# GNN layer, output stage: TensorE's waits of a block gathered in one place, layer 2 with 512 moving columns

## The reference

```python
msgs_f = mlp2(concat(h[src], h[dst], edge), W1_f, b1_f, W2_f, b2_f)
msgs_r = mlp2(concat(h[dst], h[src], edge), W1_r, b1_r, W2_r, b2_r)
agg = segment_sum(msgs_f, dst) + segment_sum(msgs_r, src)
out = x + h + relu(concat(agg, h) @ Wn1 + bn1) @ Wn2 + bn2
```

## Time and profile before

| | us |
|---|---|
| time before, median of 3 executions (1595.52 to 1598.82) | 1595.94 |
| the profiled execution's own time | 1595.95 |
| its span, first to last instruction | 1594.2 |
| output stage, first table transpose to the end of the span | 1341.1 to 1594.2 |
| TensorE busy over the span | 1280.9 (80%) |

### The profile page before, as it was taken

How to read it: one execution, slowest core, us unless ns; L and a number is a source line. 1 busy time by engine, 2 the same in 40 slices (tenths; PEclk the granted TensorE clock), 3 DMA queues, 4 the chain that set the end, 5 groups by cost and what they waited for, 6 DMA issues and landing times.

```text
span 1594.2 us, 29478 instructions
## 1 busy us (share of the span) xinstructions
PE 1280.9 (80%) x7070; PEld 969.6 (61%) x7070; DVE 970.8 (61%) x3294; ACT 942.6 (59%) x2256; POOL 1102.0 (69%) x1003
## 2 busy tenths in 40 slices
PE   5998998557888787878777788778678873999998
PEld 4777776335666565666555566556566652777776
DVE  7999999526666666666666666666666650222222
ACT  4888888434555455555455555555555442777776
POOL 7888888888888888888888888888888863000000
PEclk9999999767777888787888877877977786999999
DMA  6899998535555555555555555555555545999998
GB/s 217 292 315 315 314 315 279 161 49 111 111 112 111 111 99 102 104 104 103 105 105 105 105 104 99 106 102 99 101 102 105 104 78 156 382 370 369 364 367 297
DMA packets 238410, 281.00 MB, mean 176 GB/s; under 512 B 53170, under 2 KB 155200, under 8 KB 238348
## 3 DMA queue, kind: packets, MB, share of 16 engines
q1 hardware_dynamic: 168408, 241.57, 45.3%
q0 software_dynamic: 68992, 38.59, 21.5%
q10 hardware_dynamic: 948, 0.30, 0.1%
HBM read 162.62 MB, written 117.72 MB: 176 GB/s over the span
## 4 chain that ended last, share of the span: by engine, by line
POOL 36%; issue 21%; PE 18%; DMA 2%; DVE 1%; POOLq 1%; ACT 0%; ACTq 0%; DVEq 0%; SPq 0%
POOL table L532 30%; PE bank L871 6%; PE bank L882 6%; POOL got_odd L514 6%; PE bank L892 3%; DMA table<-to_send,scatter_at 2%; PE bank L820 1%; PE bank L846 1%; PE bank L818 1%; DVE same L979 0%; PE bank L833 0%; DMA same<-table 0%; ACT nh L639 0%; ACT to_send L625 0%; POOLq L530 0%
## 5 line engine op out<-in xcount | busy, mean ns | idle before, releaser
L532 POOL DMA_INDIRECT table<-to_send,scatter_at x392 | 623.5, 1591 | 134.7 <-issue 117.8
L846 PEld LDWEIGHTS bank<-message,same 128*128 128x128 f32 x1960 | 279.1, 229 | 45.6 <-issue 40.4
L846 PE MATMUL bank<-message,same 128*128 128x128 f32 x1960 | 300.2, 320 | 5.0 <-DVE message L1011 5.0
L639 ACT ACTIVATE nh<-nx,all_sums,all_rstd 128x64 f32<-128x64 f32 x784 | 280.3, 434 | 0.0
L514 POOL DMA_INDIRECT got_even<-in_x,gather_first x196 | 211.8, 1080 | 40.2 <-issue 35.0
L775 PE MATMUL bank<-wn_h,nturned 128*128 128x256 f32 x784 | 197.0, 395 | 31.7 <-ACT nhidden L683 24.1
L514 POOL DMA_INDIRECT got_odd<-in_x,gather_at x180 | 180.3, 1002 | 54.9 <-issue 54.9
L804 PE MATMUL bank<-ident,h_ends 128*128 128x128 f32 x196 | 51.4, 355 | 200.5 <-DVE h_ends L1020 185.6
L979 DVE TENSOR_SCALAR_CACHE_REDUCE same<-others,ids 128x128 f32<-128x128 int32 (+3 forms) x392 | 190.8, 543 | 12.7 <-DVE ids L971 7.5
L818 PE MATMUL bank<-turned,w_ends 128*128 128x256 f32 x392 | 167.8, 518 | 34.8 <-ACT turned_edge L609 34.8
L775 PEld LDWEIGHTS bank<-wn_h,nturned 128*128 128x128 f32 x784 | 143.5, 193 | 67.7 <-issue 37.9
(11 more groups left out here) (80 smaller groups left out, 1999.2 us busy)
## 6 DMA issues: line engine op xcount, KB each, us to landing
nx<-in_x SPq DMA_DIRECT2D x194, 256.0 KB
table<-nhidden SPq DMA_DIRECT2D x97, 512.0 KB
same<-table SPq DMA_DIRECT2D x97, 512.0 KB, 5.3
others<-numbers SPq DMA_DIRECT2D x196, 128.0 KB
out_x<-nh SPq DMA_DIRECT2D x79, 256.0 KB, 4.4
nx<-out_x SPq DMA_DIRECT2D x55, 256.0 KB, 4.4
out_x<-ncentred SPq DMA_DIRECT2D x49, 256.0 KB, 4.2
table<-to_send,scatter_at POOLq DMA_INDIRECT x392
```

The source lines that it names most:

```text
L532: pool.indirect_dma_start(table, bass.IndirectOffsetOnAxis(ap=scatter_at[s][:, k:k + 1], axis=0), to_send[s][:, k, :], None, compute_op=AL ...
L639: last = act.activation(nh[s][:, g, :], nx[place][:, g, :], ACT.Relu, bias=all_sums[:, at, g:g + 1].rearrange("p a g -> p (a g)"), scale=a ...
L846: last = pe.matmul(bank[6 + s][:, k * M:(k + 1) * M], same[s][:, o, k * P:(k + 1) * P], message[s][:, o, :], start=(o == k), stop=(o == KB ...
```

## The change

Nothing but TensorE's program of the output stage is changed. The table transposes of a block are now written at the end of the step before it, all waits of a step stand in front of the back transposes, and the second layer takes 512 moving columns in two matmuls where it took 256 in four. The first table transposes stand ahead of the loop.

```diff
             def turn_table(i, s, turn, place):
-                pe.wait_ge(n_tab[place], 16 * (turn + 1))
-                if not first(i):
-                    pe.wait_ge(n_hidden[s], 2 * i)
                 for odd in range(2):
...
             def layer2_nodes(i, s):
-                if not first(i):
-                    pe.wait_ge(n_biased[s], i)
-                pe.wait_ge(n_hidden[s], 2 * (i + 1))
-                for c in range(0, 512, 256):
-                    for odd in range(2):
-                        last = pe.matmul(bank[s][odd * D:(odd + 1) * D, c:c + 256], wn2[:, :],
-                                         nhidden[s][:, odd * 512 + c:odd * 512 + c + 256], start=True, stop=True)
+                for odd in range(2):
+                    last = pe.matmul(bank[s][odd * D:(odd + 1) * D, :], wn2[:, :],
+                                     nhidden[s][:, odd * 512:(odd + 1) * 512], start=True, stop=True)
                 last.then_inc(n_l2[s], 1)

             def turn_back(i, s):
-                pe.wait_ge(n_biased[s], i + 1)
-                if not first(i):
-                    pe.wait_ge(n_out[s], i)
                 for q in range(G // 2):
...
+            def wait_biased(i, s):
+                pe.wait_ge(n_biased[s], i + 1)
+                if not first(i):
+                    pe.wait_ge(n_out[s], i)
+
+            def wait_hidden(i, s):
+                pe.wait_ge(n_hidden[s], 2 * (i + 1))
+
+            def wait_table(i, s, turn, place):
+                pe.wait_ge(n_tab[place], 16 * (turn + 1))
+
             def window(w):
-                w.do(turn_table, ring=NRING)
+                w.do(wait_biased, -2)
+                w.do(wait_hidden, -1)
+                w.do(wait_table, 1, ring=NRING)
                 w.do(turn_back, -2)
                 w.do(layer2_nodes, -1)
-
+                w.do(turn_table, 1, ring=NRING)
+
+            wait_table(0, 0, 0, 0)
+            turn_table(0, 0, 0, 0)
             run(pe, NW, [(4, 96, 4)], 2, window)
```

More of the change, by code:

```diff
@@ L875, in layer2_nodes @@
             def layer2_nodes(i, s):
-                if not first(i):
-                    pe.wait_ge(n_biased[s], i)
-                pe.wait_ge(n_hidden[s], 2 * (i + 1))
-                for c in range(0, 512, 256):
-                    for odd in range(2):
-                        last = pe.matmul(bank[s][odd * D:(odd + 1) * D, c:c + 256], wn2[:, :],
-                                         nhidden[s][:, odd * 512 + c:odd * 512 + c + 256], start=True, stop=True)
+                for odd in range(2):
+                    last = pe.matmul(bank[s][odd * D:(odd + 1) * D, :], wn2[:, :],
+                                     nhidden[s][:, odd * 512:(odd + 1) * 512], start=True, stop=True)
                 last.then_inc(n_l2[s], 1)
             def turn_back(i, s):
+                for q in range(G // 2):
+                    last = pe.transpose(bank[6 + s][:, q * P:(q + 1) * P], nturned[s][:, q * P:(q + 1) * P], ident[:, :])
+                last.then_inc(n_back[s], 1)
+            def wait_biased(i, s):
                 pe.wait_ge(n_biased[s], i + 1)
@@ L890, in turn_back @@
                     pe.wait_ge(n_out[s], i)
-                for q in range(G // 2):
-                    last = pe.transpose(bank[6 + s][:, q * P:(q + 1) * P], nturned[s][:, q * P:(q + 1) * P], ident[:, :])
-                last.then_inc(n_back[s], 1)
+            def wait_hidden(i, s):
+                pe.wait_ge(n_hidden[s], 2 * (i + 1))
+            def wait_table(i, s, turn, place):
+                pe.wait_ge(n_tab[place], 16 * (turn + 1))
             def window(w):
-                w.do(turn_table, ring=NRING)
+                w.do(wait_biased, -2)
+                w.do(wait_hidden, -1)
+                w.do(wait_table, 1, ring=NRING)
                 w.do(turn_back, -2)
                 w.do(layer2_nodes, -1)
+                w.do(turn_table, 1, ring=NRING)
+            wait_table(0, 0, 0, 0)
+            turn_table(0, 0, 0, 0)
             run(pe, NW, [(4, 96, 4)], 2, window)
```

## The result

The changed kernel takes **1625.03 us** (median of 4 runs, 1623.77 to 1626.87), the kernel before 1595.73 beside it: ratio 1.0184, 95% interval 1.0171 to 1.0196. It is slower by 29 us, where +16 was forecast. The time lies just above the range, which ended at 1624.

The account below looks back on a forecast made before the run. A TensorE-ScalarE ring through the bias was taken to fill each 2.505 us step, loads close behind. Two rings, not added, gave +0.16 a step: 15.4 over 96 steps, about 1 for first blocks, hence 1612 us (8 in 10: 1593 to 1624).

Parts of the forecast that it names:

- part 5: Output stage: table's wait, moved 1.60 us earlier, comes before the table lands; +0.1 us a step, bounds none to 0.25.
- the sum: Output stage: each step takes the later of two rings, not both added; +0.16 us a step, +16 us in all.
- second ring: Back transposes of a block, store, table load, landing, back transposes three steps on: 7.8 us, or 2.61 a step.
- Parts 1, 2 and 3: Output stage: unchanged order, waits leaving second layer and table transposes (bounds 0 and 0.15 a step), 512-column matmuls: each 0.
- the ring of the bias: TensorE's back transposes and second layer, ScalarE's bias, next back transposes: sum 2.53 us, one step.
- Part 6: Start and end of the output stage: first four tables land before their turn, tail order is the same; 0.
- Part 4: Waits executed behind the bias's wait, ahead of the back transposes, lengthen the bias's ring: +0.13 us a step (0 to 0.19).
- No change: Rival: sequencer reads waits ahead and landings shift to fit; 0 a step, 1593 to 1599 us, chance 0.16.
- The gaps were the waits': Rival: 0.15 us a step ahead of the second layer goes with the waits; 1582 us, chance 0.13.
- Two halves stop overlapping: Rival: second layer's 512-column matmuls take one pass longer, 0.43 us a step; +54, 1650 us, chance 0.06.
- Landings alone bind harder: Rival: late table landings cost 0.25 us a step; 1620 us, inside the forecast range, no chance of its own.
- steps near 2.66: Sign named for the output stage: a step near 2.66 us from the second layers' starts, against 2.505 before.

Follow-up runs that it names:

- k5: Kernel before with only the table's wait moved ahead of the preceding back transposes: 1624.11 us, ratio 1.0185.
- k3: Kernel before with only the second layer's two matmuls of 512 columns in place of four of 256: 1593.95 us, ratio 0.9996.
- k10: Changed kernel with tables loaded one step earlier and every group done for two blocks at once: 1580.62 us, ratio 0.9909.
- k12: Changed kernel with tables loaded one step earlier and each wait back ahead of its own group: 1593.19 us, ratio 0.9990.
- k4: Changed kernel with tables loaded one step earlier, waits still gathered: 1605.8 us, ratio 1.0075.
- k9b: Changed kernel with the table's load issued ahead of the `x + h` load: 1613.5 us, ratio 1.0113.
- k11b: Kernel before with two more, long satisfied waits ahead of the back transposes: 1598.65 us, ratio 1.0018.

## Why the prediction was wrong in size

The direction was right, and so was the mechanism of each ring. The step that failed is part 5 with the sum: the term "second ring, +0.1 a step", worked out from the mean lateness of two tables and spread over three steps, and "the mean lies over both, +0.16". The runs showed instead a ring that is closed by the worst of the four tables, once in four steps, and whose landing grew: the table's wait by itself is +0.33 a step (k5), all of the 29 us.

*Parts 1, 2 and 3* (order none, gaps 0, 512 columns 0) held: k3 is level, and the gaps are 1.01 and 0.53 to 0.59 in the changed kernel, with the waits gone from there. The gap is the array's change of shape (k10, and the rows of the node stage). Part 2 read some 0.15 ahead of the second layer; it is 0.09, and the rest of the 0.58 was the late start of 0.05. In the ring of the bias the prediction calls ScalarE idle in the 1.21 from second layer to bias; its row says 0.26 of them, and the sum is untouched. *Part 6* held too: the stage began 1.1 us earlier, for reasons ahead of it, and the tail was as before.

*Part 4* forecast +0.13 a step, from 0.5 over four steps. Measured between k12 and k4, where nothing else binds: 0.124, from 0.50 over four. But in the changed kernel it costs next to nothing on top of part 5 (1625.03 with it, 1624.11 in k5, which has only the table's wait moved): as said there, the two rings are not added.

*Part 5* had the ring's members right, and its 0.05 from landing to transposes too. Three things were wrong.

First, which block closes it. I read the loads of two neighbouring blocks, 0.7 and 0.1 late, and took the mean with the median landing, 0.25. But the four steps of the loop differ: in the kernel before the tables land, on average, 0.63, 0.11, 0.55 late and 0.03 early against the new place. The one with 0.63, issued 2.77 after the back transposes three steps back, was not among those I read. A pipeline with a late table in one step waits the whole of that lateness there; the stall then lets the next three land in time (0.6 to 1.0 us ahead), so the others' earliness is no credit. The worst decides, not the mean. It was the next load behind the two that I read, in the kernel before on SyncE's queue, with its time to landing, and the back transposes it has to be there for:

```profile
1454.33 0.36 SPq L392 DMA_DIRECT2D out_x<-nh  x1
1454.88 0.33 SPq L386 DMA_DIRECT2D nx<-out_x  x1
1455.43 0.33 SPq L386 DMA_DIRECT2D same<-table  x1
...
DMA to landing us min/median/max: 5.2/5.2/5.2
...
1460.20 0.60 PE L892 MATMUL bank<-ident,nturned 128*128 128x128 f32 x4
```

1455.43 - 1452.66 = 2.77, and 1455.43 + 5.2 = 1460.6 is 0.4 late; the mean of this place is 0.63.

Second, the fourth step. A ring over three steps closes only where that one table comes round, once in four; the step behind the stall is its own length, and that one is stretched by part 4, from 2.48 to 2.73 (to 2.64 in k5, by the table's own wait). So over four steps, averaged over the records of either kernel:

- before: 2.77 to the issue + 5.40 landing - 0.63 (the table lands that much after these back transposes, which don't wait for it) + 2.48 = 10.02
- after: 2.77 + 5.86 landing + 0.05 from landing to the transposes + 2.73 = 11.41

These add up to the measured steps by the way they are taken; that the ring closes is shown by the 0.05, which is the same in all 17 rounds from 1413 to 1600 us. Two of these landings in the chain that ended last, in the changed kernel, with the start and length of each:

```profile
1445.67 5.79 DMA same<-table
...
1456.99 6.25 DMA same<-table
```

The transposes behind them start at 1451.50 and 1463.29.

Third, the sizes inside. The difference of 1.39 is 0.63 of lateness, 0.46 of longer landing, 0.05 of release (as I took it) and 0.25 of the stretched step. Lateness alone, by the worst step, would have given 0.63 / 4 = 0.16 a step; the other 0.76 is what the change did to its own ring. That is why even the upper bound of part 5, 0.25, was too low. I had allowed landings to shrink with less traffic; they didn't. Why they grew at the table that is waited for stays open. The same store and `x + h` load stand ahead of it at the same distances (0.56 and 1.10 after; 0.55 and 1.10 before), so these alone can't be it. In k9b, with the `x + h` load behind, it takes 5.50, but before it takes 5.40 with the load ahead.

*The rivals.* "No change" fell with the result: the interval of the ratio, 1.0171 to 1.0196, is far from 1. "The gaps were the waits'" fell: gaps as before. "Two halves stop overlapping" fell with k3. "Landings alone bind harder", 1620, was nearest in time and in kind.

Of the signs named beforehand, these came: idle time ahead of L880 released by the load, none ahead of L874 and L868, unchanged gaps, the records of L874 in pairs (here 0.48 apart in the first pair, 0.43 was named), everything before 1341 us much the same. These didn't: steps near 2.66, and landings at or under 5.2. Next to no idle time released by the bias shows either (one wait of 0.5 us from 1400 to 1550): records of transposes are longer than their distance, so the late start at 1454.22 leaves hardly a gap in the timeline.

## What to carry to other kernels

Before a wait is moved earlier, set the landing of what it waits for against the new place in each step of the loop and take the worst, not the mean: the others give nothing back, and the period is the ring that closes where the worst one comes round, over the steps in it. Where waits are gathered, the one fulfilled last belongs at the end, and the sequencer's instructions in the trace, not the code, show how many still stand behind it. Here each put off the group in its step by 0.08 to 0.1 us on a ring without slack, while those ahead were free. The gain in this stage lay elsewhere, in fewer changes of the array's shape, which pairs of blocks give.

## What the runs showed that I had not expected

- Time to landing didn't fall with the load on the DMA engines: 5.2 us at 366 GB/s before, 5.3 at 326 GB/s after, 5.0 at 350 GB/s in k4 (medians, 1400 to 1550 us).
- A place of waiting that was 0.63 us too early in one step of four cost 1.39 us per four steps: the ring that it closed grew while it bound.
- Several waits can share one instruction, and then cost as one (k11b: two added waits, 0.034 us a step).
- The table that is waited for landed later than in the kernel before (5.86 us against 5.40), the one of the last place in the loop sooner (4.74 against 4.96).
